# Graph attention's edge loop: the batch chain behind the row products one step later, rows weighed 11 steps behind their scores instead of 10

## The reference, cut to what matters

```python
s = x_l[src] + x_r[dst] + e_feat                 # one row of 4 x 64 for each edge
s = leaky_relu(s, 0.2)
alpha = einsum('ehc,hc->eh', s, att)             # a score for each edge and head
amax = segment_max(alpha, dst, num_segments=n)
ex = exp(alpha - amax[dst])
denom = segment_sum(ex, dst, num_segments=n)
alpha = ex / (denom[dst] + 1e-16)
out = segment_sum(alpha[..., None] * x_l[src], dst, num_segments=n)
```

## Time and profile before

| what | us |
|---|---|
| median of 3 runs without a profile | 3181.06 |
| lowest and highest of them | 3168.73 to 3182.11 |
| span of the profiled execution, first to last instruction | 3452.9 |

### The profile page before, as it was taken

One profiled execution on the slowest core, in us unless ns is written; L12 is line 12 of the kernel. 1 busy time (PEld: TensorE's weight loads), 2 busy tenths in 40 slices (PEclk: granted clock), 3 DMA queues, 4 the chain that ended last, 5 costly groups with the idle time before them and its releaser, 6 DMA issues. The chain is left out here.

```text
span 3452.9 us, 50836 instructions
## 1 busy us (share of the span) xinstructions
PE 3048.3 (88%) x13612; PEld 2420.6 (70%) x13613; DVE 1834.2 (53%) x3643; ACT 1508.7 (44%) x4936; POOL 1189.9 (34%) x1152
## 2 busy tenths in 40 slices
PE   6678888788888888884999999999999999999999
PEld 5456656566565665563778877877787888888898
DVE  5566666666676666676754564374365435111103
ACT  2067666777667676775322322232231212222232
POOL 4556555565555655630310031030021001222210
PEclk9899899999999999997999999999999988999999
DMA  7556655555665655554211011100001032333361
GB/s 217 152 148 148 145 145 141 143 144 141 149 145 145 147 142 150 136 94 124 52 38 37 27 30 31 41 8 1 15 27 50 1 100 84 128 120 119 119 176 38
DMA packets 288628, 345.06 MB, mean 100 GB/s; under 512 B 155176, under 2 KB 213655, under 8 KB 284512
## 3 DMA queue, kind: packets, MB, share of 16 engines
q1 hardware_dynamic: 232813, 174.79, 19.1%
q0 software_dynamic: 53632, 157.89, 17.6%
q10 hardware_dynamic: 2064, 10.81, 1.0%
HBM read 298.03 MB, written 44.37 MB: 99 GB/s over the span
## 5 line engine op out<-in xcount | busy, mean ns | idle before, releaser
L1470 POOL DMA_INDIRECT a_g<-xl_d,a_ix x480 | 468.1, 975 | 311.6 <-issue 116.0
L1504 PE MATMUL b_pM<-b_m,b_oh 128*112 128x281 f32 x1680 | 513.6, 451 | 28.5 <-DVE g_acc L1644 22.5
L1599 ACT ACTIVATE b_m<-a_g,c_pcx 128x64 f32<-128x64 f32 x1856 | 460.4, 334 | 33.6 <-issue 33.6
L1504 PEld LDWEIGHTS b_pM<-b_m,b_oh 128*112 128x112 f32 x1680 | 327.6, 200 | 156.7 <-issue 69.0
L1470 POOL DMA_INDIRECT XS<-xl_d,a_ix x344 | 333.3, 969 | 216.5 <-issue 91.1
L1637 DVE SCALAR_TENSOR_TENSOR a_r<-a_pS,g_attx 128x528 f32<-128x528 f32 x420 | 286.6, 699 | 198.4 <-remote 91.6
L1599 ACT ACTIVATE b_m<-XS,c_pcx 128x64 f32<-128x64 f32 x1424 | 351.5, 333 | 14.3 <-issue 14.2
L2286 ACT ACTIVATE f_hid<-f_pH,f_b 128x256 f32<-128x256 f32 (+3 forms) x360 | 161.9, 451 | 423.0 <-PE f_pH L2180 409.9
L450 PE MATMUL m_pH<-m_h,m_w 128*128 128x313 f32 (+1 forms) x1280 | 342.3, 426 | 4.5 <-DVE m_h L612 4.5
L125 POOL TENSOR_TENSOR m_rstd<-m_ve,m_mhalf 125x5 f32<-125x5 f32 x41 | 48.0, 1170 | 801.5 <-DVE m_ve L111 801.5
L1497 PE MATMUL a_pS<-g_xr,a_lt 128*128 x840 | 237.1, 406 | 97.8 <-ACT a_pS L1581 60.8
(11 more groups left out here) (413 smaller groups left out, 4629.2 us busy)
## 6 DMA issues: line engine op xcount, KB each, us to landing
a_db<-dl_d SPq DMA_DIRECT2D x212, 224.0 KB
f_w<-in_ffn_W1p SPq DMA_DIRECT2D x16, 1024.0 KB
wide_w<-in_ffn_W1p SPq DMA_DIRECT2D x16, 1024.0 KB
m_w<-in_mix_W SPq DMA_DIRECT2D x8, 1024.0 KB
f_w<-in_ffn_W2p SPq DMA_DIRECT2D x8, 1024.0 KB
a_g<-xl_d,a_ix POOLq DMA_INDIRECT x480
a_lt<-eat_d SPq DMA_DIRECT2D x214, 32.0 KB
eat_d<-a_stage SPq DMA_DIRECT2D x15, 448.0 KB
```

What stands on the lines that cost most here:

```text
L1470: p.indirect_dma_start(out=gathered(t)[:, j, :], out_offset=None, in_=xl_d, in_offset=bass.IndirectOffsetOnAxis(ap=IX[:, t // BSTEPS, n:n ...
L1504: ins = pe.matmul(pM[0:WN, h, 0:MW], OH[:, b, j, :], M[:, b, j, :], start=(j == 2 * h), stop=(j == 2 * h + 1))
L1599: ins = a.activation(m[:, j, part], gathered(ts)[:, j, part], ACT.Copy, scale=of[:, first + j, h, 0:1])
```

## The change

`WEIGH, SUM, ADD` become 11, 12, 13. The tail becomes 13 steps. All links of the chain behind the row products move one step: the row scans from the end of tau 0 to tau 1 (where the rescans stood, behind the one-hot `OH`), the column products, copy, rescans and maximum to tau 2, and so on to the scaling of the accumulator at tau 6. Since the parity of a weighed step's buffer is no longer that of t, buffers are named by `(t - WEIGH) % 2`. Nothing is added or taken out.

```diff
--- before.py
+++ after.py
@@ -53,7 +53,7 @@
 LTS = BSTEPS
 EA0 = GD
 MW = EA0 + ED + 1
-WEIGH, SUM, ADD = 10, 11, 12
+WEIGH, SUM, ADD = 11, 12, 13
 AHEAD = 3
 SLOPE = 0.2
 LOW = -float(2 ** 100)
@@ -1431,7 +1431,7 @@
                                 breaks_of(2 * i + t // BSTEPS, t // BSTEPS)
                         if exists(base, t, -WEIGH):
                             wait(sp, "b_summed1", base, t - WEIGH - 1)
-                            sp.dma_start(M[:, t % 2, :, EA0:EA0 + ED], ea_d[four(base, t - WEIGH), :].rearrange("i (e c) -> e i c", c=ED)).then_inc(s[f"b_ea{t % 2}"], 16)
+                            sp.dma_start(M[:, (t - WEIGH) % 2, :, EA0:EA0 + ED], ea_d[four(base, t - WEIGH), :].rearrange("i (e c) -> e i c", c=ED)).then_inc(s[f"b_ea{(t - WEIGH) % 2}"], 16)
 
                     rounds(sp, slot)
                     tail(slot)
@@ -1517,7 +1517,7 @@
                         if tau == 0:
                             wait(pe, "a_alpha", base, t)
                             pe.transpose(pA[0:CP, 0:TE], AX_[:, par, :, :].rearrange("p h i -> p (h i)"), ident[:, :]).then_inc(s["c_turned"], 1)
-                        elif tau == 3:
+                        elif tau == 4:
                             pe.wait_ge(s["c_p"], n)
                             pe.wait_ge(s["c_cl"], n)
                             for d in range(2):
@@ -1526,7 +1526,7 @@
 
                         if scoring:
                             scores_of_second(ws)
-                        if tau == 1:
+                        if tau == 2:
                             pe.wait_ge(s["c_rowscan"], n)
                             for d in range(2):
                                 ins = pe.matmul(pY[0:CP, 240 + d:241 + d], ST[0:1, par, d, d:d + CP], one[:, :], start=True, stop=True)
@@ -1553,10 +1553,10 @@
                         if summing:
                             sums(1)
 
-                        if tau == 2:
+                        if tau == 3:
                             pe.wait_ge(s["c_diff"], n)
                             pe.matmul(pA[0:1, 0:GH], FB[:, 0, 0:1], by_item(ident[0:CP, 0:CP])[:, :, 0], start=True, stop=True).then_inc(s["c_new"], 1)
-                        elif tau == 4:
+                        elif tau == 5:
                             pe.wait_ge(s["c_fade"], n)
                             row = OH[0:1, (t - SUM) % 2, 0, :]
                             pe.matmul(pA[0:WN, 0:GH], row, fade[:, :], start=True, stop=False)
@@ -1579,17 +1579,17 @@
                                 a.wait_ge(s[f"a_g{t}"], rows_landed(i, t))
                             wait(a, "a_gated1", base, t)
                             a.activation(pS[0:TE, 2:4, 0:GD], gathered(t)[:, 2:4, :], ACT.Copy).then_inc(s["a_filled"], 1)
-                        if tau == 3:
+                        if tau == 4:
                             a.wait_ge(s["c_back"], n)
                             a.activation(PCX[:, par, :, :, :].rearrange("p i h d -> p d h i"),
                                          pY[0:TE, 256:256 + 2 * CP].rearrange("p (d h i) -> p d h i", d=2, h=GH)[:, :, :, 0:BI], ACT.Copy).then_inc(s["c_pcx"], 1)
                             a.wait_ge(s["c_pcx"], n)
-                        elif tau == 4:
+                        elif tau == 5:
                             a.wait_ge(s["c_less"], n)
                             a.activation(fade[:, :], fade[:, :], ACT.Exp).then_inc(s["c_fade"], 1)
                         if exists(base, t, -WEIGH):
                             ts = (t - WEIGH) % RING
-                            of, m = PCX[:, ts // BSTEPS, :, :, :], M[:, t % 2, :, :]
+                            of, m = PCX[:, ts // BSTEPS, :, :, :], M[:, (t - WEIGH) % 2, :, :]
                             first = IG * (ts % BSTEPS)
                             wait(a, "b_summed1", base, t - WEIGH - 1)
                             a.activation(m[:, :, 0:GD].rearrange("p i (h d) -> p i h d", h=GH)[:, :, :, HD:GW], of[:, first:first + IG, :, :], ACT.Copy)
@@ -1647,7 +1647,7 @@
                             q = base + (t - ADD)
                             both = v.value_load(WP[0:1, (slice(q, q + 1) if isinstance(q, int) else bass.ds(q, 1))], min_val=0, max_val=1023)
                             at = [v.snap((both & 31) * MW), v.snap((both >> 5) * MW)]
-                        if tau == 5:
+                        if tau == 6:
                             v.wait_ge(s["c_scale"], n)
                             wait(v, "b_added1", base, t - ADD)
                             w = flat[:, bass.ds(at[0].with_bounds(min_val=0, max_val=(NW - 1) * MW), GD)].rearrange("p (h d) -> p h d", h=GH)[:, :, 0:HD + 1]
@@ -1660,12 +1660,12 @@
                             v.memset(ACC[:, at_w:at_w + CLEAR_W, :], 0.0).then_inc(s["b_zeroed"], 1)
                         elif at_start(i) and t == ADD:
                             v.wait_ge(s["b_zeroed"], len(CLEARED))
-                        if scoring and tau == 5:
+                        if scoring and tau == 6:
                             onehot(i + (t + 1) // RING, (t + 1) % RING)
                             v.wait_ge(s["c_faded"], n)
                         if adding:
                             add(0, at)
-                        if scoring and tau != 5:
+                        if scoring and tau != 6:
                             onehot(i + (t + 1) // RING, (t + 1) % RING)
                         if adding:
                             add(1, at)
@@ -1677,10 +1677,10 @@
                             v.wait_ge(s[f"c_breaks{par}"], 96 * i + (0 if odd else 96))
                             v.tensor_tensor_scan(FB[:, 0, :], BR[:, par, 0, :], scores, LOW, ALU.add, ALU.max)
                             v.tensor_tensor_scan(FB[:, 1, ::-1], BR[:, par, 1, ::-1], scores[:, ::-1], LOW, ALU.add, ALU.max).then_inc(s["c_scan"], 1)
-                        elif tau == 2:
+                        elif tau == 3:
                             v.wait_ge(s["c_max"], n)
                             v.tensor_tensor(FB[:, 1, :], scores, FB[:, 0, :], ALU.subtract).then_inc(s["c_diff"], 1)
-                        elif tau == 3:
+                        elif tau == 4:
                             v.wait_ge(s["c_new"], n)
                             v.tensor_tensor(fade[:, :], by_item(ST[0:1, 1 - par, 0, 0:CP])[:, :, BI], pA[0:1, 0:GH], ALU.subtract).then_inc(s["c_step"], 1)
                         if scoring:
@@ -1691,23 +1691,29 @@
                             v.wait_ge(s["c_pcx"], (STEPS + t - WEIGH) // BSTEPS + 1)
                             wait(v, "b_summed1", base, t - WEIGH - 1)
                             heads_of = lambda r: r.rearrange("p i (h d) -> p i h d", h=GH)[:, :, :, 0:HD]
-                            v.tensor_tensor(heads_of(M[:, t % 2, 2:4, 0:GD]), heads_of(gathered(ts)[:, 2:4, :]),
+                            v.tensor_tensor(heads_of(M[:, (t - WEIGH) % 2, 2:4, 0:GD]), heads_of(gathered(ts)[:, 2:4, :]),
                                             PCX[:, ts // BSTEPS, first:first + 2, :, 0:1].broadcast_to([TE, 2, GH, HD]), ALU.mult).then_inc(s["b_shared"], 1)
                         if weighing:
                             wait(v, "b_summed1", base, t - WEIGH - 1)
-                            v.tensor_tensor(OH[:, t % 2, :, :], nodes[:, :].unsqueeze(1).broadcast_to([TE, IG, WN]),
+                            v.tensor_tensor(OH[:, (t - WEIGH) % 2, :, :], nodes[:, :].unsqueeze(1).broadcast_to([TE, IG, WN]),
                                             DLX[:, four(base, t - WEIGH)].unsqueeze(2).broadcast_to([TE, IG, WN]), ALU.is_equal).then_inc(s["b_onehot"], 1)
                         if tau == 1:
+                            v.wait_ge(s["c_rows"], n)
+                            for d, way in enumerate((1, -1)):
+                                ins = v.tensor_tensor_scan(ST[0:1, par, d, 0:CP][:, ::way], ANY[0:1, par, d, :, :].rearrange("p h i -> p (h i)")[:, ::way],
+                                                           pY[0:1, d * CP:(d + 1) * CP][:, ::way], LOW, ALU.add, ALU.max)
+                            ins.then_inc(s["c_rowscan"], 1)
+                        elif tau == 2:
                             v.wait_ge(s["c_cols"], n)
                             v.tensor_copy(IN[:, :], pY[0:CP, 240:242]).then_inc(s["c_init"], 1)
                             v.wait_ge(s["c_init"], n)
                             v.sem_inc(s["c_seen"], 1)
                             v.tensor_tensor_scan(FB[:, 0, :], BR[:, par, 0, :], scores, IN[:, 0:1], ALU.add, ALU.max)
                             v.tensor_tensor_scan(FB[:, 1, ::-1], BR[:, par, 1, ::-1], scores[:, ::-1], IN[:, 1:2], ALU.add, ALU.max).then_inc(s["c_rescan"], 1)
-                        elif tau == 2:
+                        elif tau == 3:
                             v.scalar_tensor_tensor(out=PC[:, 1, :], in0=BR[:, par, 1, :], scalar=1.0 / LOW, in1=FB[:, 0, :],
```

(10 more changed lines are left out.)

## The result

| | us |
|---|---|
| before, median of 4 runs | 3180.36 (3168.73 to 3182.11) |
| changed, median of 4 runs | 3251.59 (3247.38 to 3258.23) |
| changed / before | 1.0239, 95% interval 1.0215 to 1.0264 |

The change makes the kernel 2.4% (71 us) slower; the forecast was 3183 us with a range up to 3225. The span of the profiled execution is 3256.5 us, and its own time 3258.23.

The account below looks back on a forecast made before the run. The prediction took all engines as near 32 to 37 us a batch, with GpSimd's gathers at 36.3 us and few waits unprofiled. Terms 0 + 0 + 0 + 0 + 2.2 us on 3181.1 gave 3183 us, range 3140 to 3225.

Parts of the forecast that it names:

- The bound: Edge loop: all engines near 32 to 37 us a batch, GpSimd's gather issues at 36.3 us; the rest is waits.
- The 272 us: Profiled span minus unprofiled median, all taken from the edge loop: 1136 us unprofiled, at most 51 us of waits left.
- Parts 1 to 3: Row scans, column products and the later chain links each move one step: gain or loss 0.
- Part 5: One more tail step without a chain behind the loop: +2.2 us.
- Part 4: Weighing 11 behind: GpSimd's gathers wait up to one ScalarE step (4.47 us) longer, data 0.0 to 2.9 us late; taken as 0.
- the slower rival: Gathers become the bound through the ring wait: 17 to 41 us, middle 29 us, 3212 us; chance 0.30.
- sign of being wrong: Forecast is wrong if batches shrink by over 1 us or fills wait for gathers in every batch.
- The landing: Gathered data arrives 4.17 us after the last issue; 7.11 us only behind the staged tiles' store, once in 14 steps.
- What a late landing costs: A fill waiting for late gathered data costs its lateness, 2.9 us, once in each of 14 rounds.
- The cover of 1.7 us: Ring release comes 13.3 us after ScalarE's step's first gather; GpSimd needs 15.0 us for three steps, leaving 1.7 us.
- The rule on branches: Loop head's wait 3.3 us longer than the middle's, 46 us over 14 rounds, belongs to the branch and stays.
- The faster rival: TensorE's signal lag exists unprofiled; VectorE does an accumulation and one-hot during it: 27 us, 3156 us; chance 0.27.

Follow-up runs that it names:

- again_before: The kernel before, unchanged, profiled once more on a chip A: span 3163.9 us, profiled time 3165.62 us; measured 3170.31 us, ratio 0.9992.
- experiment 2: The kernel before with only GpSimd's gathers waiting for the weighing of one step more, chip A: 3246.64 us, ratio 1.0229.
- experiment 3: The kernel before with weighing, sum and add at 11, 12, 13, chain left up to the PCX copy, chip A: 3256.95 us, ratio 1.0271.
- experiment 7: The changed kernel unchanged, beside the kernel before: chip A 3251.91 us, ratio 1.0232; chip B 3559.93 us against 3436.74, ratio 1.0356.
- experiment 5: The changed kernel with its two staging gathers issued at t = 2 and t = 3: chip A 3214.52 us, ratio 1.0112; chip B ratio 1.0420.
- experiment 6: The changed kernel with both staging gathers at t = 9 and their store at t = 12, chip A: 3262.06 us, ratio 1.0270.
- before_stage_split: The kernel before with its two staging gathers issued at t = 2 and t = 3, on a chip B: ratio 1.0010.

## Why the prediction was wrong

**The bound.** That GpSimd's issues set the pace, 36.3 us a batch, agrees with `again_before`: odd batches, with no staging gathers (35.0 us of issues), take 36.0 us, and even ones, with two (37.6 us), take 39.2.

**The 272 us.** The prediction put them down to the profiler. They are the chip's: 3452.9 us was a normal time of a chip B. The conclusion drawn for a chip A, that few waits are left there, held all the same: 1408 - 272 = 1136 us was forecast for the loop and `again_before` shows 1132.5. The reason given was wrong, so the size is right by luck.

**Parts 1 to 3**, the moved links at 0: consistent on chip A with experiments 2 and 3, which give the whole loss without them. On chip B the long steps are elsewhere with the moved links (experiment 7), at a price that no run separates. Part 5, one tail step of 2.2 us, is in the noise of a single comparison.

**Part 4 is the step that failed.** Mechanism and place were named (the ring's release one ScalarE step later, fills that wait for landings), but it was taken at 0, and as the slower rival at 29 us. It measured 64 to 81 us (experiment 2, 0.0203 to 0.0256 of 3173 us). The prediction's own sign of being wrong came true: fills wait for gathers in every batch, at t = 1 and 2 of the even ones and at t = 8 of the odd ones. Two of its terms were mis-sized:
- *The landing.* I took 4.17 us as usual and 7.11 us as an event beside SyncE's store, at t = 5. The place to look at was GpSimd's own queue: the gathers of t = 2 stand behind 896 KB of staging gathers, and land 7.51 us after the last issue in the place shown, 7.1 to 9.1 in the 14 rounds. No fill waits at t = 5. I had counted the staging gathers' 1.26 us of issue and not the bytes that they put in front of the next gathers. Experiments 5 and 6 show it: with the gathers apart half the loss is gone, and with the gathers at t = 9 the long step is there.
- *What a late landing costs.* I took 2.9 us for one, the lateness itself. The step became 12.9 - 7.3 = 5.6 us longer in the median, and 4.6 on average over the 14 rounds. In the place shown TensorE, idle for 4.91 us, came back at half its clock for the scores that everyone waited for.

The cover of 1.7 us that I set against it was worked out with the usual landing; with 7.5 us in place of 4.17 the same sum is 16.7 us against 15.0, and the cover is gone where it was needed. The trace agrees: the first gather of t = 5 starts 850.39 - 833.55 = 16.8 us after that of t = 2, held by the weighing for 2.08 us.

**The rule on branches.** From the longer wait at a round's head I took the Trainium skill's rule (Runtime: NRT & Kernel Launch, "Instruction fetch mechanics"), that a taken branch out of the fetched window stalls the engine for a fetch, as a possible reason. For the stall near the head of a round on chip A experiment 6 excludes it: the stall follows the staging gathers. In `again_before` the steps across the branch, t = 13 to 0 and 0 to 1, take 4.9 and 6.3 us, as their twins from 6 to 7 and 7 to 8 do, so no cost of the branch shows. For the difference of 7.98 and 4.66 us on chip B it was not tried.

**The faster rival** fell in experiment 7, on the very kind of chip that it was made for.

## What to carry to other kernels

When a ring's reader moves back by one step, count it as a step less of lead for whoever refills the ring, and test that lead against the worst landing that something waits for, not the usual one; here it was that of the gathers that stand behind the largest ones in their own queue. A tiny edit of the wait alone (experiment 2) prices this in one run. And compare the span of a profile with the unprofiled times before reading it: here a gap of 8.5% meant that the profile showed the waits of another kind of chip.

## What the runs showed that I had not expected

**Two kinds of chip.** The same kernel took 3173 and 3176 us on one chip at two times and 3175 us on a second; it took 3461 and 3437 us on two others, each met once. No chip showed both times, but with four chips this does not prove that a chip keeps its kind. In the profiles of the second kind engines that wait for TensorE's signals idle up to 10.5 us, released by no recorded work near it in time, in the edge loop and not in the stages behind it (waits of a chip B, `before_stage_split`, 158 to 1528 us):

```profile
ACT b_m L1596 <- remote: 179.2, 39, 10.5
...
DVE c_state L1722 <- remote: 119.2, 26, 8.5
```

The loop is where DMA is busy (0.58 of the 16 engines in the earlier trace rows, against 0.20 behind it). The Trainium skill (Perfetto Trace Analysis, "Per-instruction lifecycle") places a signal's way outside the recorded window, and the trace agrees: the product recorded at 866.69 us is followed by what waits for it only at 876.38. Busy DMA alone does not make the lag, since in `again_before` the loop's share is higher, 0.75, and no such idle is there. Why one kind of chip has it stays open.

**An edit's gain can depend on the chip.** The split staging gathers take 1.2% off the changed kernel on chip A (1.0232 to 1.0112, on the same chip). On one chip B it stood at 1.0420 and the changed kernel on another at 1.0356, so no gain is seen there. That it hurts is not shown, as the two never ran on one chip B together.
